# A two-attention decoder layer: the turn between cross heads reordered, and the cross query biases moved behind the first normalisation

## The reference

```python
x = layernorm(x + self_attention(x))              # 1024 x 1024 scores for each of 16 heads
x = layernorm(x + cross_attention(x, ctx, mask))  # 1024 x 6404 scores; mask == 0 -> -1e9
x = layernorm(x + ffn(x))                         # router over 8 experts, the best one's product
```

## Time and profile before

| what | value |
|---|---|
| median of 3 runs | 510.89 us (509.74 to 511.15) |
| the profiled execution | 509.33 us, its span 507.6 us |
| PE busy | 482.6 us, 95% of the span |
| DVE busy | 426.1 us, 84% |
| ACT busy | 358.9 us, 71% |
| POOL busy | 199.6 us, 39% |
| mean granted PE clock | 0.993 |

### The profile page before, as it was taken

How to read it: one execution, slowest core, us unless ns; L and a number is a source line. 1 busy time by engine, 2 the same in 40 slices (tenths; PEclk the granted TensorE clock), 3 DMA queues, 4 the chain that set the end, 5 groups by cost and what they waited for, 6 DMA issues and landing times.

```text
span 507.6 us, 13805 instructions
## 1 busy us (share of the span) xinstructions
PE 482.6 (95%) x4140; PEld 197.3 (39%) x4140; DVE 426.1 (84%) x633; ACT 358.9 (71%) x685; POOL 199.6 (39%) x305
## 2 busy tenths in 40 slices
PE   7989999999999999888999999999999999999892
PEld 2423333333333344633444444444444444425550
DVE  5899999999999926769999899999999999902688
ACT  6238888888888877350878888888878888885220
POOL 3615898888894000132333333333333333220010
PEclk9999999999999999999999999999999999999998
DMA  3389998787500012525234111101101111011001
GB/s 96 83 264 324 305 332 295 257 299 285 224 23 13 12 54 71 178 68 147 51 62 81 41 40 39 41 26 40 38 28 40 29 41 40 26 56 48 0 0 45
DMA packets 21771, 52.56 MB, mean 104 GB/s; under 512 B 5022, under 2 KB 13376, under 8 KB 19650
## 3 DMA queue, kind: packets, MB, share of 16 engines
q1 hardware_dynamic: 18461, 22.46, 16.9%
q0 software_dynamic: 2304, 28.84, 15.1%
q10 hardware_dynamic: 932, 0.37, 0.3%
HBM read 42.10 MB, written 8.94 MB: 101 GB/s over the span
## 4 chain that ended last, share of the span: by engine, by line
PE 80%; DVE 10%; ACT 4%; issue 3%; DMA 2%; ACTq 0%; DVEq 0%; POOL 0%; POOLq 0%
PE O L1224 30%; PE ST L1452 14%; PE RT L1424 10%; PE ST L1255 9%; PE RT L1241 5%; PE RT L1564 2%; ACT prob L1047 2%; DVE mxs L746 2%; DVE mxc L896 2%; DMA Qs<-mxr 1%; PE O L1195 1%; DVE x L943 1%; DVE stat L826 1%; PE O L1220 1%; PE ST L1142 1%
## 5 line engine op out<-in xcount | busy, mean ns | idle before, releaser
L896 DVE TENSOR_REDUCE mxc<-RT 128x1024 f32 (+1 forms) x192 | 196.2, 1045 | 18.4 <-PE RT L1424 14.0
L1087 ACT ACTIVATE prob<-ST 128x512 f32<-128x512 f32 x320 | 172.0, 596 | 34.4 <-PE ST L1452 32.8
L1047 ACT ACTIVATE prob<-ST 128x512 f32<-128x512 f32 x256 | 138.6, 597 | 26.3 <-PE ST L1255 15.6
L746 DVE TENSOR_REDUCE mxs<-RT 128x2 f32<-128x1024 f32 x128 | 153.3, 1224 | 4.4 <-PE RT L1241 2.2
L1424 PE MATMUL RT<-Kr,Qs 64*128 64x128 f32 (+1 forms) x512 | 120.7, 372 | 1.9 <-DVE mxc L896 1.2
L1452 PE MATMUL ST<-Qs,Kc 64*128 64x512 f32 x320 | 120.5, 453 | 0.7 <-ACT prob L1087 0.7
L1224 PE MATMUL O<-prob,vst 128*9 128x256 f32 x1280 | 99.1, 381 | 1.6 <-ACT prob L1087 1.3
L1241 PE MATMUL RT<-Kself,Qs 64*128 64x512 f32 x256 | 89.2, 450 | 3.1 <-DVE Kself L713 1.4
L1255 PE MATMUL ST<-Qs,Kself 64*128 64x512 f32 x256 | 91.2, 450 | 0.3 <-DMA Qs<-mxr 0.3
L1224 PE MATMUL O<-prob,Vs 128*9 128x256 f32 x1024 | 79.3, 381 | 1.5 <-ACT prob L1047 0.7
L1452 PEld LDWEIGHTS ST<-Qs,Kc 64*128 64x128 f32 x320 | 53.8, 185 | 58.7 <-issue 29.9
(11 more groups left out here) (224 smaller groups left out, 344.5 us busy)
## 6 DMA issues: line engine op xcount, KB each, us to landing
big<-in_mask POOLq DMA_DIRECT2D x16, 1760.0 KB, 7.8
big<-kd SPq DMA_DIRECT2D x66, 80.0 KB
od_s<-osb SPq DMA_DIRECT2D x14, 128.0 KB, 3.4
od_x<-osb SPq DMA_DIRECT2D x14, 128.0 KB, 1.8
Qs<-qd_s SPq DMA_DIRECT2D x12, 128.0 KB, 7.2
Qs<-qd_x SPq DMA_DIRECT2D x12, 128.0 KB, 3.8
qd_s<-Vx SPq DMA_DIRECT2D x2, 512.0 KB, 3.7
qd_x<-big SPq DMA_DIRECT2D x2, 512.0 KB, 4.7
```

The source lines that it names most:

```text
L746: v.tensor_reduce(mxs[:, h % 2, c2, :].rearrange("p (f t) -> p f t", f=2)[:, :, q], RT[r % 2][:, :].rearrange("p (f k) -> p f k", f=2), AX ...
L896: v.tensor_reduce(o, src, AX.X, ALU.max).then_inc(S("x_row_free"), 1)
L1047: nc.scalar.activation(prob[:, c % SLOTS, k * HALF:(k + 1) * HALF], ST[(2 * c + k) % 3][:, :], ACT.Exp) \
L1087: nc.scalar.activation(prob[:, b, (k % 2) * HALF:(k % 2 + 1) * HALF], ST[BANK[k]][:, :], ACT.Exp) \
```

## The change

Five edits:

1. PE: the branch for the turn between heads is gone. A turn now goes as inside a head: `have_max`, column 0, rows 4, column 1, rows 4, values 4 of the head in front, rows 5, then `clear_o`.
2. ACT: `copy_o` of the head in front stands behind the first exponential of the new head.
3. DVE: `first_bias("x")` stands behind the normalisation; PE waits for it (`bias_moved`) before the query products of head 1.
4. PE: three constant products between the two groups of four transposes, in the self attention's `project_out` only.
5. ACT reads `p0` in the loop of the self attention before block 126 of 128, not behind its end. The stores of the first pair count on `pen_out` in place of `kd_out`, which starts at 64.

```diff
@@ sync
+            sp.sem_inc(S("kd_out"), 64)
...
-            def k_out(c, key, k):
+            def k_out(c, key, k, name="kd_out"):
...
-                                 (kx_hi[c][:, :].bitcast(F32), kx_lo[c][:, :])[b // 2]).then_inc(S("kd_out"), 16)
+                                 (kx_hi[c][:, :].bitcast(F32), kx_lo[c][:, :])[b // 2]).then_inc(S(name), 16)
...
-                k_out(0, slice(KPAD - PAIR, KPAD), k)
+                k_out(0, slice(KPAD - PAIR, KPAD), k, "pen_out")
...
-            sp.wait_ge(S("pen_out"), 16)
+            sp.wait_ge(S("pen_out"), 80)
@@ vector
-                if a == "s":
-                    dve.wait_ge(S("bias_ready"), 2)
-                    first_bias("x")
-                    settle()
-                    dve.sem_inc(S("bias_moved"), 1)
...
             project_out("s")
+            dve.wait_ge(S("bias_ready"), 2)
+            first_bias("x")
+            settle()
+            dve.sem_inc(S("bias_moved"), 1)
@@ scalar
-                    act.wait_ge(S("pen_out"), 16)
+                    act.wait_ge(S("pen_out"), 80)
...
+                if c == 126:
+                    p0 = act.snap(act.value_load(steer[0:1, 0:1], min_val=0, max_val=NP - MIN_PAIRS))
...
-            p0 = act.snap(act.value_load(steer[0:1, 0:1], min_val=0, max_val=NP - MIN_PAIRS))
...
+                step_exp(T0, 0)
                 if g:
                     copy_o("x", g - 1, act.snap(T0 * NBLK + NBLK))
-                step_exp(T0, 0)
                 step_exp(T0, 1)
@@ tensor
                     mm.then_inc(S(a + "_xT"), 1)
+                    if a == "s" and h == 0:
+                        warm_up(ST[2], 3)
...
                 for h in range(DIRECT):
+                    if h:
+
+                        pe.wait_ge(S("bias_moved"), 3)
                     half_q0("x", h, f)
...
-                    if g != g_before and not first:
-
-                        if h < HEADS:
-                            rows(1, 4, h, U)
-                            rows(0, 4, h, U)
-                        values(g_before, T_before, NBLK - 1, e + NCOL)
-                        have_max("x", g)
-                        for f in range(2):
-                            col(g, T, f, e + (NCOL + 1 + f - AGAIN[f]))
-                            if h < HEADS:
-                                for q in (2, 3):
-                                    rows(1 - f, 5, h, U, [q])
-                        return
+                    if first and h < HEADS:
+                        rows(1, 4, h, U)
                     if g != g_before:
-                        if h < HEADS:
-                            rows(1, 4, h, U)
                         have_max("x", g)
                     col(g, T, 0, None if first else e + (NCOL + 1 - AGAIN[0]))
-                    if g == g_before and h < HEADS:
+                    if not first and h < HEADS:
                         rows(1, 4, h, U)
                     col(g, T, 1, None if first else e + (NCOL + 2 - AGAIN[1]))
```

## The result

The changed kernel takes 514.12 us, the median of 17 runs (510.43 to 519.15), beside 511.15 us of the kernel before in the 17 runs shown with it. The ratio is 1.0049, its 95% interval 1.0026 to 1.0072; runs with a mean granted clock of 0.976 and less are left out of it. The change made the kernel slower, by half a per cent. The forecast was 509.4 us with 507.0 to 511.5 around it, and gave "slower" 0.11.

The account below looks back on a forecast made before the run. The prediction took PE's chain as the bound (80% PE, DVE 10%). Gains of 0.95 (edits 1, 2) and 0.54 (edit 3) less 0.10 (edit 5) made 1.39, plus 0.15 for rounding, 1.5: 510.89 to 509.4 us, range 507.0 to 511.5.

Parts of the forecast that it names:

- the sum for edits 1 and 2: Turns between cross heads: 0.05 us gained at each of fourteen, 0.25 at the last, 0.95 us together.
- Block 4's values move to 266.98 + 1.21 = 268.19: At a cross-head turn, block 4's values start 1.21 us behind block 3's, as inside a head, 0.21 later than before.
- the term of 0.93: At a turn, the new head's first values come 0.93 us behind clear, as seen at the start of head 0.
- The rival on the maxima: At turns, maxima landing over 2.13 us behind issue delay column 0; each 0.1 us beyond costs 1.5 us; chance 0.08.
- Copy at 0.69, clear 0.42 behind it, clear waiting at all turns: At turns, ACT's copy starts 0.69 us behind block 4's values, clear 0.42 behind the copy, PE waiting 0.19.
- The last turn: Turn to head 15: clear to first values falls from 1.18 to 0.93 us, gaining 0.25, bounds 0 to 0.5.
- Edits 3, 4, 5: Between the attentions: edit 3 gains 0.54 us, edit 4 costs nothing, edit 5's register load costs 0.10.
- Only the middle pays: Rival: the turns give nothing, only edits 3 and 5 count, -0.54 + 0.10, 510.4 us; chance 0.27.
- Clock: Rival: a half-clock stretch appears in the middle (near 511.1 us, 0.06) or goes from the end (507.7 us, 0.07).
- POOL's operation and the second bias operation: Between the attentions: long L695 ends with POOL's operation; edit 5 alone would free it; moved bias operations cost nothing.

Follow-up runs that it names:

- experiment 3: Changed kernel with the four row products of half 1 ahead of the wait for the maxima and column 0 at a turn; ratio to before 1.000.
- experiment 4: Changed kernel with ACT copying cross heads 0 to 14 from another tile and clear not waiting; one run, last to first values 1.84 us, heads 217.57 us.
- x_rest_only: Changed kernel with edits 1 and 2 taken back, so edits 3, 4, 5 alone; 509.57 us, ratio to before 0.9963.
- x_start_flag: Rows ahead of the wait, first pass written out, clear dropped for cross heads, first values overwriting by start flag, against the changed kernel; 506.97 us, ratio to before 0.9919.
- x_start_exp1: The start-flag kernel with ACT's copy of O behind exponential 1 of the new head in place of exponential 0; 507.08 us, ratio to before 0.9911.
- x_late_clear: Changed kernel with rows ahead of the wait, clear moved to just before the new head's first values, first pass written out; 509.58 us, ratio to before 0.9973.
- x_old_order_start: The start-flag kernel with the turn order of the kernel before, for PE and for ACT's copy; 515.68 us, ratio to before 1.0089.

## Why the prediction was wrong

The failed step is in the sum for edits 1 and 2, "Block 4's values move to 266.98 + 1.21 = 268.19", with what it rests on: that a wait which is fulfilled before column 0 is due costs nothing. The step measured 1.20 to 1.53 us, mean 1.35. This is half of the miss at the turns; the other half is the term of 0.93 in the same sum, taken from a clear at which PE doesn't stand. The rival on the maxima had the right place and the wrong price: it asked for a landing within 2.13 us, found 1.83, and would have closed. What counts is that PE's queue reaches the wait before the maxima have landed, 0.27 behind block 3's values, and has its register instructions still to do. Point by point:

- **Block 3's to block 4's values**: 1.21 forecast, 1.35 the mean of fourteen, 2.0 us in all. Shown by experiment 3, which has the same landing and 1.20.
- **Copy at 0.69, clear 0.42 behind it, clear waiting at all turns**: right (0.69, 0.43, 14 times).
- **Clear to first values 0.93**: 1.06, 1.8 us in all. The row was of a clear at which PE doesn't stand. The turns of the kernel before had 1.10 (269.18 to 270.28), where the first values waited for ACT, and the forecast didn't use them. Shown by experiment 4, in one run: 0.93 as soon as clear doesn't wait.
- **The last turn**: 0.46 gained, 0.25 forecast, inside its bounds.
- **Edits 1 and 2**: -0.95 forecast, +2.8 in the profile, +2.5 alone.
- **Edits 3, 4, 5**: -0.44 forecast, -0.5 to -0.7 at equal clock, -1.9 (-0.9 to -2.9) by the ratio. Edit 3's part is 1.81 to 1.29, that is 0.52 for a forecast of 0.54; edit 4 nothing; edit 5's load no cost. The parts were right; the slack for `qd_x`, worth 0.85 us where the maxima of head 0 come late, was not in it.
- **"Only the middle pays"**: this is what `x_rest_only` is, and it needs the old turns.
- **Clock**: nothing appeared in the middle of the changed kernel; of the thirteen profiles one (`x_start_flag`) has a half-clock stretch of 3.4 us near 205 us. The tail's stretch goes between none, 3.4 and 6.8 us by itself, a scatter of 2.7 us between executions that is as large as all that was argued about. The forecast had only the case that the stretch goes, and priced it at 1.7; it is worth 1.0.
- **POOL's operation and the second bias operation**: right, and shown by more than the forecast had. The bias operation took 0.99 us beside POOL's subtraction; it takes 0.29 away from it, and the same operation at 8.6 us in the kernel before, with POOL not beside it, also took 0.29. In the four profiles that have both operations as before it starts 0.5 to 0.9 us behind POOL's start, takes 0.71 to 1.05 us, and ends 0.02 or 0.03 us behind POOL's end each time. That agrees with the rule of the Trainium skill (GPSIMD Engine Reference, section 1, Specifications) that the forecast names, a contention of POOL and DVE at their shared SBUF interfaces. No run has edit 5 without edit 3. An estimate from the rows: POOL's operation now ends 0.25 us behind the projection's start (208.60 + 1.54 - 209.89) and the bias operation stood 0.58 behind it (209.88 - 209.30), so edit 5 alone would have freed it.

The turn had a gain in it: `x_start_flag` is 6.8 us shorter in the heads than the changed kernel and 3.9 shorter than the kernel before. Of the 6.8 the rows ahead of the wait gave 2.1, the later clear 2.2 and the start flag 2.5. The order of the columns gave nothing by itself, but with the old order the missing clear left the turn at 3.32.

## What to carry to other kernels

A wait can cost although its data land before the array needs them, when the engine's queue reaches it earlier and has register instructions to do behind it. Put products that need nothing from it right ahead, as here the four row products, worth 2 us over 14 turns. Before reordering around a wait, ask which instruction truly needs what is waited for, and move or drop the one that waits for the others' sake. A duration taken from a place without a stall can be too short for the same products behind one, here 0.93 for 1.06.

## What the runs showed of the hardware

- Where PE's queue stood at a semaphore, products behind it came later than where it didn't: by 0.13 to 0.33 us behind the maxima at 11 of 14 turns of the changed kernel, by 0.13 behind the clear.
- A transfer of 8 KB from SBUF to SBUF on SP's queue landed 1.81 to 1.85 us behind its issue, at all turns of the changed kernel.
- A register load of ACT beside its exponentials took 0.30 us, where the same load behind them had taken 1.13.
- The half-clock stretches in the tail come in lengths of 3.4 and 6.8 us or not at all, whatever the edits, and cost 1.0 and 2.7 us; comparing runs of the same mean granted clock takes this out.
- A program of PE written out for one more pass had stops of about 1 us, each of which ended 1.25 to 1.53 us behind the end of a 16 KB packet of the instruction queue q8 (`x_start_flag`, `x_start_exp1`, `x_late_clear`, `x_old_order_start`), and one of them (1.24 us, in the last) was followed by 3.4 us at 1.2 GHz.
- An operation of DVE on 128x2 elements beside one of POOL ended within 0.03 us of POOL's end in four of four profiles, up to 0.76 us longer than the 0.29 it took elsewhere.
